# Two-layer attention kernel on one core: the hi and lo parts of the setup's products and the first statistics take other places in the engines' queues

## The chip, the core and the metric

The kernel runs on one core of one Trainium2 chip. The metric is the device time of one execution in microseconds (us); the median of several executions is compared. The engines named in the profile are PE (TensorE, matrix products; PEld is its weight load), ACT (ScalarE), DVE (VectorE), POOL (GpSimd) and SP (SyncE, which issues all the transfers here). Each engine works through its own queue of instructions in program order and waits at semaphores. Memory on the chip is SBUF (128 partitions) and PSUM, to which TensorE writes.

## The reference, cut to what matters

The input x is 8 x 512 x 32 x 32, in float32. Two attention layers follow each other:

```python
# layer 0
hn = group_norm(x, gn1_scale, gn1_bias)              # 32 groups of 16 channels
qkv = einsum('bchw,oc->bohw', hn, w_qkv) + b_qkv     # 8 heads of 64 channels, 1024 positions
a = softmax(q^T k / sqrt(64)) v                      # per batch element and head
x = x + group_norm(einsum(a, w_proj) + b_proj, gn2_scale, gn2_bias)
# layer 1
w_qkv, w_out = g * v / norm(v, axis=1)               # weight normalisation, rows
qkv = einsum('oc,bcn->bon', w_qkv, x); qkv = qkv / (rms over channels + 1e-4)
h = softmax(q^T k * 512**-0.5) v                     # one head of 512 channels
out = (x + einsum('oc,bcn->bon', w_out, h)) / sqrt(2)
```

## The kernel before, in words

**Arithmetic.** Large products are made from split operands: a float32 value is stored as a hi part, rounded by a copy to the type float32r, and a lo part, which is the value minus the hi part. A product then takes three passes, hi x hi, hi x lo and lo x hi. ScalarE makes hi parts and VectorE lo parts, so each split is two instructions on two engines, the second waiting for the first.

**The loop.** After a setup, eight batch elements run one after the other in `body(b, last)`. Each engine has such a body with the same steps. TensorE projects q and k (line 560), then v, runs 64 score steps with transposes and values around them, the output projection, and the products of layer 1. The body of the change's kernel is the same.

**The setup on TensorE** (lines 451 to 479) makes three products of the weights of layer 1, each in four units `i = 0..3` of 128 rows, in plain float32, which TensorE takes as two instructions per matmul in the trace:
- first product (line 458): v_qkv blocks 8 to 11 with wo, 8 instructions of 512 columns a unit. Unit 0 and 1 go at once; unit i from 2 on waits for `s_prod_lo >= i - 1`, that is for the lo part of unit i - 2, which frees the buffer `big[i % 2]`.
- second product (line 465): blocks 0 to 3 with 4 to 7, also 8 instructions a unit. It first waits for all 12 weight blocks to be normalised; unit i waits for `s_prod_lo >= 3 + i`.
- the group means of the first x (line 469), which wait for `s_gn_mean >= 1`, the end of the channel statistics.
- third product (line 473), 24 instructions a unit, narrower from unit to unit (512, 384, 256, 128 columns); unit i waits for `s_prod_lo >= 7 + i`. After its unit 0 come the group variances (lines 444 and 446).
Before the first body TensorE waits for all twelve lo parts and for the normalised x.

**The setup on ScalarE** (lines 759 to 796): the sums of squares of the weight blocks 8 to 11, then of blocks 0 to 7 (`square_sums`, line 746), then `product_hi(0)`, four pairs of q/k weight splits (line 772, two instructions each), `product_hi(1)`, the two long splits of the v and output weights into W0 and W1 (line 778), `product_hi(2)`, `product_hi(3)` and so on. `product_hi(i)` (line 748, its instruction at line 754) waits for unit i, counted over all three products, and copies the hi part out of PSUM.

**The setup on VectorE** (lines 1041 to 1139): the scaling of blocks 8 to 11, `product_lo(0)` (line 1048, its instruction at line 1053), the scaling of blocks 0 to 7 (line 1065), which waits for GpSimd's power of all twelve sums of squares (line 942), then four pairs of q/k lo parts (line 1072), `product_lo(1)`, the lo parts of W0 and W1 (line 1080), `product_lo(2)`, `product_lo(3)`, `product_lo(4)`. Then it waits for x (`s_x_next`) and makes the channel statistics of four blocks (lines 1087 to 1090, three instructions each), with `product_lo(5)`, `(6)` and `(7)` after the first three. Group means, variances and coefficients, the normalised x (line 1110) and its lo part (line 1116) follow.

**SP's queue** (lines 312 to 350, then its body): the loads of the weights; after `s_split_lo >= 4` the load of x into XA (line 327), whose space held the q/k weights; after `s_split_lo >= 6` the load of v_out (line 329), then the stores of the first group (d_qk[0], d_wp and, after the first product, d_u, line 338). SP waits for these, reloads the first q/k weights (line 340) and stores the second group (d_wv, the other d_qk, d_m). It waits for that group (line 346), stores d_g (line 349), waits for it, and goes on to its body: the second q/k weights (line 372) and the stack loads (`stack_head`, line 364), which wait for the q and k of the batch (`s_nat_ready`) and which the first scores wait for. One stack is six loads of 256 KB.

```python
pe.wait_ge(s_prod_lo, i - 1)              # first product, unit i >= 2 (line 457)
pe.wait_ge(s_prod_lo, KB + i - 1)         # second product, unit i (line 463)
group_means(1, ops[0][:, 0:KB], every, None, s_gn_first)     # line 469
pe.wait_ge(s_prod_lo, 2 * KB + i - 1)     # third product, unit i (line 471)
sp.wait_ge(s_split_lo, PAIRS)             # ahead of the load of x (line 326)
```

Of the kernel before, what the change touches and what calls it, by code (L numbers as in the profile page):

```python
# [20 lines left out]
KB = C // P  # L21
# [12 lines left out]
ACT = mybir.ActivationFunctionType  # L34
# [50 lines left out]
def build(nc, x, wv_t, wp_t, wqk_t, v_qkv, v_out, wo_t, vecs, consts, out):  # L85
    ctx = ExitStack()
    with ctx:
        def sb(name, shape, dt=f32):
            return ctx.enter_context(nc.sbuf_tensor(name, shape, dt))
# [4 lines left out]
        def sem(name):  # L94
            return ctx.enter_context(nc.semaphore(name))
# [9 lines left out]
        X = sb("X", [P, KB, N])  # L105
# [7 lines left out]
        W = [sb("W0", [P, 4096], f32r), sb("W1", [P, 4096], f32r)]  # L113
# [68 lines left out]
        s_split_hi = sem("split_hi")  # L182
# [81 lines left out]
        def w1_block(j, start=0, stop=HALF):  # L264

            return PB[:, j // 2, HALF * (j % 2) + start:HALF * (j % 2) + stop]

        def qk_part_of(tile, part):

            return tile.rearrange("p (k n) -> p k n", k=KB)[:, :, P * part:P * part + P]  # L270

        def wqk_stage(i):
            return XA[:, (2, 3, 0, 1)[i], :]

        def product_stage(i):

            return (ST[:, 4:8, :].rearrange("p a n -> p (a n)"), PT[:, :, :, :].rearrange("p a h n -> p (a h n)"),
                    ST[:, 0:4, :].rearrange("p a n -> p (a n)"))[i]

        def product_parts(i):  # L280

            k = i % KB
            if i // KB == 0:
                return [(slice(0, HALF), 1.0)]
            if i // KB == 1:
                return [(slice(0, HALF), SCALE1)]

            return [(slice(P * k, P * k + P), 1.0)] + ([(slice(P * k + P, HALF), 2.0)] if k < KB - 1 else [])
# [451 lines left out]
        def _(act):  # L740
            act_fn = nc.scalar.activation

            def square_sums(n, src, col):
                if n > 1:
                    act.wait_ge(s_square_sum, n - 1)
                act_fn(RB[:, 0:HALF], src, ACT.Square, accum_out=ssq[:, col:col + 1]).then_inc(s_square_sum, 1)

            def product_hi(i):
                act.wait_ge(s_big_full, i + 1)
                if i == 2 * KB:  # L750
                    act.wait_ge(s_const_set, 1)
                for cols, factor in product_parts(i):
                    at = HALF * (i % KB)
                    last = act_fn(product_stage(i // KB)[:, at + cols.start:at + cols.stop], big[i % 2][:, cols],
                                  ACT.Copy, scale=factor)
                last.then_inc(s_prod_hi, 1)
# [6 lines left out]
            act.wait_ge(s_in_l1, 8 * 16)  # L763
            for j in range(8):
                square_sums(j + 5, w1_block(j), j)
            for i in range(PAIRS):
                if i == 0:
                    product_hi(0)
                if i % 2 == 0:
                    act.wait_ge(s_in_qk[i // 2], 32)  # L770
                for part, factor in ((0, SCALE0), (1, 1.0)):
                    last = act_fn(qk_part_of(VT[:, 2 * i, :], part), qk_part_of(wqk_stage(i), part),
                                  ACT.Copy, scale=factor)
                last.then_inc(s_split_hi, 1)
            product_hi(1)
            act.wait_ge(s_in_l0, 32)
            for w, src in ((W[0], X[:, 0:2, :]), (W[1], X[:, 2:4, :])):
                act_fn(w[:, 0:2048], src.rearrange("p a n -> p (a n)"), ACT.Copy).then_inc(s_split_hi, 1)
            product_hi(2)
            product_hi(3)  # L780
            for i in range(KB):
                product_hi(KB + i)
            act.wait_ge(s_in_vout, 16)
# [246 lines left out]
        def _(dve):  # L1030
# [4 lines left out]
            def link(instruction):  # L1035

                instruction.then_inc(s_dve_step, 1)
                links[1] += 1
                dve.wait_ge(s_dve_step, links[0] + links[1])
# [8 lines left out]
            def product_lo(i):  # L1048
                dve.wait_ge(s_prod_hi, i + 1)
                for cols, factor in product_parts(i):  # L1050
                    at = HALF * (i % KB)
                    stage = product_stage(i // KB)
                    last = V.scalar_tensor_tensor(stage[:, 2048 + at + cols.start:2048 + at + cols.stop],  # L1053
                                                  big[i % 2][:, cols], factor,
                                                  stage[:, at + cols.start:at + cols.stop].bitcast(f32),
                                                  ALU.mult, ALU.subtract)
                last.then_inc(s_prod_lo, 1)

            for n, rows in ((1, range(8, 12)), (2, range(0, 8))):  # L1060
                dve.wait_ge(s_norm_pow, n)
                cols = slice(rows.start, rows.stop)
                link(V.tensor_tensor(wscale[:, cols], rnorm[:, cols], g_l1[:, cols], ALU.mult))
                for j in rows:
                    V.tensor_scalar(w1_block(j), w1_block(j), wscale[:, j:j + 1], None, ALU.mult)\
                     .then_inc(s_w_normed, 1)
                if n == 1:
                    product_lo(0)
            for i in range(PAIRS):
                dve.wait_ge(s_split_hi, i + 1)  # L1070
                for part, factor in ((0, SCALE0), (1, 1.0)):
                    last = V.scalar_tensor_tensor(qk_part_of(VT[:, 2 * i + 1, :], part),
                                                  qk_part_of(wqk_stage(i), part), factor,
                                                  qk_part_of(VT[:, 2 * i, :], part).bitcast(f32),
                                                  ALU.mult, ALU.subtract)
                last.then_inc(s_split_lo, 1)
            product_lo(1)
            for i, (w, src) in enumerate(((W[0], X[:, 0:2, :]), (W[1], X[:, 2:4, :]))):
                dve.wait_ge(s_split_hi, i + PAIRS + 1)
                V.tensor_tensor(w[:, 2048:4096], src.rearrange("p a n -> p (a n)"), w[:, 0:2048].bitcast(f32),  # L1080
                                ALU.subtract).then_inc(s_split_lo, 1)
            product_lo(2)
            product_lo(3)
            product_lo(KB)

            def channel_stats(k):
                V.bn_stats(stats[:, k, 0:6], XA[:, k, 0:HALF])
                link(V.bn_stats(stats[:, k, 6:12], XA[:, k, HALF:N]))
                own_wait(dve)
                return V.bn_aggr(mv[:, k, :], stats[:, k, :])  # L1090
# [28 lines left out]
            dve.wait_ge(s_x_next, 16)  # L1119
            for k in range(KB):  # L1120
                last = channel_stats(k)
                if k < KB - 1:
                    product_lo(KB + k + 1)
            last.then_inc(s_gn_mean, 1)
            dve.wait_ge(s_gn_mean, 1)
            dve.wait_ge(s_gn_first, 1)
            group_dev(ops[0][:, 0:KB], mv[:, :, 0], every)
# [299 lines left out]
```

## Time and profile before

| what | value |
|---|---|
| median of 3 executions | 3530.38 us |
| lowest and highest | 3525.94 and 3533.14 us |
| the profiled execution's own time | 3528.0 us |
| its span, first to last instruction | 3526.2 us |
| mean granted clock of TensorE | 0.998 |
| TensorE busy (matmuls) | 3462.6 us, 98% of the span |
| VectorE / ScalarE / GpSimd busy | 2077.1 / 1825.4 / 1083.3 us |
| first matmul of the first batch | 83.42 us |

### The profile page before, as it was taken

How to read it: one execution, taken by the hardware profiler on the slowest of the kernel's cores; microseconds unless marked ns; L12 is line 12 of the kernel's file. 1: busy time of each engine (PE TensorE's matmuls, PEld its weight loads, DVE VectorE, ACT ScalarE, POOL GpSimd, SP SyncE). 2: the span in 40 equal slices, each digit the busy share in tenths (PEclk: the TensorE clock that was granted, in tenths of full speed). 3: DMA queues.
4: the chain of work that ended last, by engine and by line, in shares of the span. 5: the costliest groups of instructions: out<-in, count | busy, mean ns of one | idle time of the engine just before them, and what ended most of it. 6: DMA issues, size and time to landing. Idle time of an engine off the chain costs nothing.

```text
span 3526.2 us, 52658 instructions
## 1 busy us (share of the span) xinstructions
PE 3462.6 (98%) x17360; PEld 2835.9 (80%) x17360; DVE 2077.1 (59%) x3388; ACT 1825.4 (52%) x3074; POOL 1083.3 (31%) x947
## 2 busy tenths in 40 slices
PE   7999999999999999999999999999999999999999
PEld 3888788887888788887878878788787887888878
DVE  4677446773377734786347854478444884457742
ACT  3577126762278522784237832378323882247822
POOL 0245213442034410354104531145211452114521
PEclk9999999999999999999999999999999999999999
DMA  8512215312244113341033311342203422142210
GB/s 310 157 39 58 108 43 138 74 48 84 66 115 96 41 69 97 85 96 72 36 121 81 76 72 43 114 96 61 84 37 109 96 61 84 43 133 65 60 48 24
DMA packets 63520, 294.41 MB, mean 83 GB/s; under 512 B 9201, under 2 KB 9457, under 8 KB 52465
## 3 DMA queue, kind: packets, MB, share of 16 engines
q1 hardware_dynamic: 63216, 290.65, 28.1%
q8 instruction: 156, 2.56, 0.3%
q14 instruction: 148, 1.20, 0.1%
HBM read 158.49 MB, written 31.46 MB: 54 GB/s over the span
## 4 chain that ended last, share of the span: by engine, by line
PE 87%; issue 6%; DVE 3%; ACT 2%; POOL 2%; DMA 0%; SPq 0%; ACTq 0%; DVEq 0%; POOLq 0%
PE big L430 29%; PE tps L529 14%; PE big L556 12%; PE ops L542 12%; PE ops L702 10%; PE big L626 6%; PE big L473 1%; PE ops L430 1%; ACT PB L827 1%; PE big L594 1%; DVE XA L1247 1%; POOL XA L967 1%; DVE HL L1252 0%; DVE small L1175 0%; PE big L465 0%
## 5 line engine op out<-in xcount | busy, mean ns | idle before, releaser
L957 POOL TENSOR_SCALAR PB<-PB,small 128x1024 f32<-128x1024 f32 x576 | 648.1, 1126 | 1304.3 <-DVE small L1181 1293.4
L833 ACT ACTIVATE PT<-tps 128x512 fp32r<-128x512 f32 x1088 | 601.2, 597 | 251.7 <-PE tps L529 248.5
L1186 DVE TENSOR_TENSOR PT<-tps,PT 128x512 fp32r<-128x512 f32 x1088 | 693.1, 678 | 39.0 <-ACT PT L833 38.6
L1175 DVE TENSOR_REDUCE small<-big 128x1 f32<-128x1024 f32 x512 | 624.8, 1220 | 63.2 <-PE big L556 59.9
L529 PEld LDWEIGHTS tps<-ident,PB 128*128 128x128 f32 x4608 | 527.1, 140 | 125.0 <-DVE PT L1186 56.0
L529 PE MATMUL tps<-ident,PB 128*128 128x128 f32 x4608 | 618.0, 275 | 8.9 <-DVE PT L1186 6.1
L827 ACT ACTIVATE PB<-big,small 128x1024 f32<-128x1024 f32 x512 | 572.2, 1118 | 73.1 <-DVE small L1175 70.2
L542 PE MATMUL ops<-PT,VT 128*128 128x512 f32 x2048 | 599.3, 415 | 0.0
L556 PE MATMUL big<-ST 128*128 128x512 f32 x2048 | 555.4, 393 | 10.9 <-ACT PB L827 10.9
L556 PEld LDWEIGHTS big<-ST 128*128 128x128 f32 x2048 | 382.1, 188 | 101.8 <-ACT PB L827 19.9
L542 PEld LDWEIGHTS ops<-PT,VT 128*128 128x128 f32 x2048 | 346.2, 189 | 47.0 <-DVE PT L1186 5.0
L430 PE MATMUL big<-HH,W 128*128 128x512 f32 x1024 | 333.9, 391 | 1.7 <-DVE ST L1053 1.1
L1167 DVE SCALAR_TENSOR_TENSOR ST<-big,vec,ST 128x512 fp32r<-128x512 f32 x128 | 96.1, 751 | 326.6 <-ACT ST L819 326.6
L819 ACT ACTIVATE ST<-big,vec 128x512 fp32r<-128x512 f32 x128 | 88.2, 689 | 303.8 <-PE big L430 303.8
L430 PEld LDWEIGHTS big<-HH,W 128*128 128x128 f32 x1024 | 192.3, 188 | 45.5 <-issue 4.4
L1322 DVE CUSTOM_DVE_ANT_0 PB<-big,RB 128x1024 f32<-128x1024 f32 x64 | 78.4, 1225 | 240.4 <-PE big L430 240.4
L967 POOL TENSOR_TENSOR XA<-RB 64x512 f32<-64x512 f32 x128 | 163.9, 1281 | 142.8 <-ACT RB L844 141.6
L1018 POOL TENSOR_SCALAR small<-small 128x1 f32<-128x1 f32 x64 | 16.9, 265 | 616.6 <-DVE small L1322 607.6
L430 PE MATMUL big<-HL,W 128*128 128x512 f32 x512 | 200.0, 391 | 0.0
L430 PE MATMUL big<-W,HH 128*128 128x512 f32 x640 | 197.1, 389 | 0.0
L702 PE MATMUL ops<-PT,VT 128*128 128x512 f32 x768 | 188.3, 394 | 0.0
L626 PE MATMUL big<-ST,W 128*128 128x512 f32 x720 | 183.2, 395 | 1.2 <-ACT XA L885 1.1
(157 smaller groups left out, 4659.2 us busy)
## 6 DMA issues: line engine op xcount, KB each, us to landing
ST<-ST SPq DMA_DIRECT2D x384, 256.0 KB, 4.9
W<-d_qk SPq DMA_DIRECT2D x32, 1024.0 KB, 5.2
XA<-in_x SPq DMA_DIRECT2D x8, 2048.0 KB, 7.7
X<-in_x SPq DMA_DIRECT2D x8, 2048.0 KB, 10.6
W<-d_wp SPq DMA_DIRECT2D x8, 2048.0 KB, 12.2
W<-d_g SPq DMA_DIRECT2D x8, 2048.0 KB, 12.2
W<-d_m SPq DMA_DIRECT2D x8, 2048.0 KB, 7.7
W<-d_u SPq DMA_DIRECT2D x8, 2048.0 KB, 10.3
```

What stands on the lines that cost most here:

```text
L430: last = mm(dst, stat(sp_, k), mov(mp_, k), start=(i == 0), stop=(i == n - 1))
L529: last = nc.tensor.transpose(tps[n % 2][:, P * t:P * t + P], PB[:, 4 * (u % 2) + t, P * s:P * s + P], ident[:])
L542: last = mm(ops[u % 2][:], VT[:, s, P * (u // 2):P * (u // 2) + P], pt_slot(u, s)[:, part, :], start=(s == 0 and part == 0), stop=(s == 7 ...
L556: last = mm(t[:, cols], stack("q", head)[:, tok:tok + P], stack(kind, head)[:, cols], start=(i == 0), stop=(i == 1))
L626: last = mm(t[:, cols], w_full[slot][:, wp, j, P * k:P * k + P], x1(xp, j)[:, cols], start=(j == 0 and i == 0), stop=(j == (k if slot == 0 ...
L702: last = mm(ops[use % 2][:], VT[:, s, col:col + P], ptb[:, pp, :], start=(s == 0 and i == 0), stop=(s == 7 and i == 2))
L827: act_fn(PB[:, i, :], t[:], ACT.Exp, bias=negmax[:, i:i + 1], accum_out=rowsum[:, i:i + 1])\
L833: act_fn(pt_slot(u, s)[:, 0, :], tps[n % 2][:], ACT.Copy).then_inc(s_pt_hi, 1)
L957: nc.gpsimd.tensor_scalar(PB[:, i, :], PB[:, i, :], rinv[:, i:i + 1], 1.0, ALU.mult, ALU.mult)\
L967: nc.gpsimd.tensor_tensor(XA[rows, pair, HALF * c:HALF * c + HALF], RB[rows, 0:HALF], RB[rows, HALF:N], ALU.add).then_inc(s_a_done, 1)
L1175: V.tensor_reduce(negmax[:, i:i + 1], tile(("s", 4 * u + tb))[:], axis=AX.X, op=ALU.max, negate=True).then_inc(s_row_max, 1)
L1186: V.tensor_tensor(pt_slot(u, s)[:, 1, :], tps[n % 2][:], pt_slot(u, s)[:, 0, :].bitcast(f32), ALU.subtract).then_inc(s_pt_ready, 1)
```

## The change

All of it lies in the setup. No instruction, wait or transfer is added or taken away. On ScalarE `product_hi(0)` goes ahead of the last three of the eight squares, `product_hi(1)` ahead of the q/k splits, `product_hi(2)` ahead of the third pair, `product_hi(3)` between the two long splits. On VectorE `product_lo(1)` goes ahead of the q/k lo parts, `product_lo(2)` ahead of the third pair, `product_lo(3)` between the long lo parts. Of the lo parts that stood between the channel statistics, one (`KB + 1`) stays, after the second block instead of the first; the other two follow the statistics.

```diff
             for j in range(8):
                 square_sums(j + 5, w1_block(j), j)
+                if j == 4:
+                    product_hi(0)
+            product_hi(1)
             for i in range(PAIRS):
-                if i == 0:
-                    product_hi(0)
+                if i == 2:
+                    product_hi(2)
                 if i % 2 == 0:
                     act.wait_ge(s_in_qk[i // 2], 32)
...
                 last.then_inc(s_split_hi, 1)
-            product_hi(1)
             act.wait_ge(s_in_l0, 32)
-            for w, src in ((W[0], X[:, 0:2, :]), (W[1], X[:, 2:4, :])):
-                act_fn(w[:, 0:2048], src.rearrange("p a n -> p (a n)"), ACT.Copy).then_inc(s_split_hi, 1)
-            product_hi(2)
+            act_fn(W[0][:, 0:2048], X[:, 0:2, :].rearrange("p a n -> p (a n)"), ACT.Copy).then_inc(s_split_hi, 1)
             product_hi(3)
+            act_fn(W[1][:, 0:2048], X[:, 2:4, :].rearrange("p a n -> p (a n)"), ACT.Copy).then_inc(s_split_hi, 1)
...
                 if n == 1:
                     product_lo(0)
+            product_lo(1)
             for i in range(PAIRS):
+                if i == 2:
+                    product_lo(2)
                 dve.wait_ge(s_split_hi, i + 1)
...
                 last.then_inc(s_split_lo, 1)
-            product_lo(1)
             for i, (w, src) in enumerate(((W[0], X[:, 0:2, :]), (W[1], X[:, 2:4, :]))):
+                if i:
+                    product_lo(3)
                 dve.wait_ge(s_split_hi, i + PAIRS + 1)
...
-            product_lo(2)
-            product_lo(3)
             product_lo(KB)
...
             for k in range(KB):
                 last = channel_stats(k)
-                if k < KB - 1:
-                    product_lo(KB + k + 1)
+                if k == 1:
+                    product_lo(KB + 1)
             last.then_inc(s_gn_mean, 1)
+            product_lo(KB + 2)
+            product_lo(KB + 3)
```

## Rows read from the trace of the kernel before

**Rows 1.** The page, its chain that ended last: shares by engine.
```profile
PE 87%; issue 6%; DVE 3%; ACT 2%; POOL 2%; DMA 0%; SPq 0%; ACTq 0%; DVEq 0%; POOLq 0%
```

**Rows 2.** Chain of waits in order of time, to 130 us: start us, us, what.
```profile
15.04 0.73 ACT RB L746 x2
...
20.31 0.73 ACT RB L746 x2
...
31.71 5.23 PE big L458 x8
36.94 13.85 PE big L465 x32
...
54.19 12.10 PE big L473 x24
...
83.42 27.52 PE big L430 x120
```

**Rows 3.** Timeline of ScalarE: start us, us, instruction, idle before and releaser.
```profile
20.94 0.58 ACT L754 ACTIVATE ST<-big 128x512 fp32r<-128x512 f32 x1
21.41 4.25 ACT L772 ACTIVATE VT<-XA 128x512 fp32r<-128x512 f32 x8
...
26.05 3.70 ACT L778 ACTIVATE W<-X 128x2048 fp32r<-128x2048 f32 x2
...
36.98 0.60 ACT L754 ACTIVATE ST<-big 128x512 fp32r<-128x512 f32 x1 [6.74 <-PE big L458]
```

**Rows 4.** Timeline of VectorE.
```profile
26.16 4.89 DVE L1072 SCALAR_TENSOR_TENSOR VT<-XA,VT 128x512 fp32r<-128x512 f32 x8
30.98 0.68 DVE L1053 SCALAR_TENSOR_TENSOR ST<-big,ST 128x512 fp32r<-128x512 f32 x1
31.58 4.47 DVE L1080 TENSOR_TENSOR W<-X,W 128x2048 fp32r<-128x2048 f32 x2
...
41.75 0.68 DVE L1087 BATCH_NORM_STATS2 small<-XA 128x6 f32<-128x512 f32 x1
...
43.17 0.21 DVE L1090 BATCH_NORM_AGGREGATE small<-small 128x2 f32<-128x12 f32 x1
```

**Rows 5.** Windows: from:to, us, PE, PEld, DVE, ACT, POOL busy, PEclk, DMA, GB/s.
```profile
31.70:34.80 3.10, 3.09 (x4) 1.51 (x5) 3.10 (x2) 0.00 (x0) 0.00 (x0) 0.50 0.79 255
...
50.60:53.80 3.20, 0.18 (x1) 0.00 (x1) 2.09 (x4) 2.89 (x8) 0.00 (x0) 1.00 0.92 394
...
55.50:58.50 3.00, 3.00 (x5) 1.35 (x4) 0.00 (x0) 0.00 (x0) 0.00 (x0) 0.50 0.35 46
```

**Rows 6.** Timeline of the weight loads, the eighth and ninth matmul of line 458 near.
```profile
16.99 0.34 PEld L458 LDWEIGHTS big<-PB 128*128 128x128 f32 x1 [0.52 <-issue]
...
18.23 0.19 PEld L458 LDWEIGHTS big<-PB 128*128 128x128 f32 x1 [0.24 <-issue]
```

**Rows 7.** Timeline of SP's issues.
```profile
31.08 0.38 SPq L327 DMA_DIRECT2D XA<-in_x  x1
...
83.00 0.32 SPq L349 DMA_DIRECT2D d_g<-ST  x1
89.51 0.32 SPq L372 DMA_DIRECT2D W<-d_qk  x1
96.21 13.46 SPq L364 DMA_DIRECT2D ST<-ST  x12
```

**Rows 8.** Transfers issued from 31 to 33 us: KB, us to landing.
```profile
XA<-in_x SPq DMA_DIRECT2D x1, 2048.0 KB, 7.9
```

**Rows 9.** The page, its DMA issues over the whole span: KB each, median us to landing.
```profile
ST<-ST SPq DMA_DIRECT2D x384, 256.0 KB, 4.9
...
X<-in_x SPq DMA_DIRECT2D x8, 2048.0 KB, 10.6
```

**Rows 10.** TensorE's waits from 300 us on, and a window behind one of them.
```profile
PE big L626 <- DVE HL L1252: 14.6, 8, 1.8
...
366.10:370.00 3.90, 3.89 (x17) 3.24 (x18) 3.15 (x2) 0.00 (x0) 3.90 (x2) 1.00 0.18 17
```

## The prediction, made before any run of the changed kernel

> **What bounds the kernel now.** I read the chain of waits first, because it tells whether time won in the setup can reach the end. TensorE is 87% of it [rows 1], and in order of time it says where the setup's length comes from [rows 2]: ScalarE's squares, the weight normalisation that hangs on them, VectorE's splits of the q/k weights up to 31.05 [rows 4], the fourth unit of the first product (TensorE, 31.71), the second product (36.94 to 50.79), then nothing on TensorE until 54.19, the third product, and the first batch from 83.42. From there TensorE hardly waits, so I take a microsecond won before 83.42 as a microsecond of the whole.
>
> So TensorE has two large holes. The first ends at 31.71. That unit needs the buffer that product_lo(1) frees. product_lo(1) stands behind eight split instructions on VectorE, and product_hi(1) behind eight on ScalarE [rows 3, 4]. The second, from 50.79, ends with the statistics of x, whose last quarter follows product_lo(7) [rows 2]. The granted clock adds a price to each hole: it is 0.50 (1.2 GHz) from 31.7 to 34.8, and again from 55.5 to 58.5, though it was still full in the hole at 50.6 to 53.8 [rows 5]. The weight loads show the two spacings: 0.85 us a matmul at the low level (the next load is at 17.80), 0.43 at 2.4 GHz (next at 18.66) [rows 6]. A unit of eight therefore takes 3.44 us, and each low stretch costs some four matmuls times 0.43, 1.7 us.
>
> **The change, step by step.** It adds no instruction and no transfer; it moves hi/lo parts and statistics. I rebuild the times with durations as spacings: ScalarE square 0.75 (15.04 to 20.31 in seven), hi part 0.47, split 0.52, long split 1.85 [rows 2, 3]; VectorE lo part 0.60, q/k split 0.60, long split 2.2 [rows 4]; a hi part starts 0.27 after its unit's last matmul; TensorE starts 0.73 after the start of the lo part that frees it (product_lo(1) starts at 30.98) [rows 2 to 4].
> 1. product_hi(0) now sits before the last three squares. The spacings put the end of unit 0 at 18.56 [rows 6], so it starts at 18.83, with ScalarE free at 18.80. It pushes the squares back 0.5, and with them the power on GpSimd and the scaling of the eight blocks: its end goes from 26.16 [rows 4] to 26.66. That is the only new wait ahead of the scaling. The gain in unit 2 is 0.3 (start 22.0 instead of 22.29, as unit 1 ends then).
> 2. product_lo(1) follows the scaling: 26.66. Unit 3 starts at 27.39, not 31.71, and ends at 30.83: 4.3 won, and 1.7 more if the clock holds over a hole of 1.95 us.
> 3. product_hi(2) waits on ScalarE until 25.7 with splits 2 and 3 queued behind it; those end at 28.25, still before VectorE asks (30.3). product_lo(2) starts at 29.67, and the second product's unit 0 at 30.83.
> 4. VectorE's q/k splits end at 32.75, 1.7 later than now (scaling 0.5, two lo parts 1.2). SP's queue stands behind them: the load of x goes out at 32.78, not 31.08 [rows 7]. It lands 7.9 later [rows 8], at 40.7.
> 5. product_hi(3) waits for unit 3 until 31.1; the copy of W1 behind it ends at 33.4, and VectorE wants it at 35.5, so it costs nothing. product_lo(3) stands behind the long split of W0: 34.91. This is a new hole: unit 1 of the second product needs it, and starts at 35.64 instead of 34.27. W1's lo part ends at 37.74, so v_out and the first stores go out about 1.75 later than now.
> 6. product_lo(4) starts at 37.74, and unit 2 runs 39.08 to 42.52. Statistics 0 and 1 wait for x: 40.7 to 43.8 (1.54 each, from the start at 41.75, the aggregate's at 43.17 and 0.12 behind it [rows 4]). product_lo(5) follows at 43.8, and unit 3 can start only at 44.5: a new hole of 2.0 us. It ends at 47.94.
> 7. Statistics 2 and 3 end at 47.5, product_lo(6) starts there. The group means and the third product start at 48.25 instead of 54.04: 5.8 won. product_lo(7), now last, ends at 49.5 and nobody needs it until TensorE's second unit of that product, near 58.5.
> 8. Without the low stretch at 55.5, the third product's unit 0 is 1.7 shorter. After it every step keeps its distance to the one before.
> Sum: 5.8 + 1.7 = 7.5 us. The first batch starts at 75.9 instead of 83.42.
>
> **What must stay hidden.** SP waits for the first stores (about 58.9 instead of 57.2), for the second group (about 82.4), then stores d_g at 82.5 (83.00 now) and issues the q/k load at 89.0 (6.5 later, as now) [rows 7]. The stack loads could start at 88.7 and start at 89.4. The first scores then want them at 103.3 (110.8 now, 14.5 behind the first issue at 96.21). Six issues at 1.12 and 4.9 to land [rows 7, 9] give 99.9; up to 2.6 more where the 1 MB q/k load (at about 400 GB/s) is still under way. That makes 102.5: covered by 0.8, a small margin.
>
> **The unknown costs.** The first is the clock. Nothing here shows my 2 us holes in the setup. The nearest row below is the wait of 1.8 us in each batch, after which the clock stays at 1.00 [rows 10]; the nearest above is the hole of 3.4 us, after which it fell [rows 2, 5]. My 2.0 lies next to 1.8, so I take no fall and keep 1.7 us as the other end. The Trainium skill (TensorE: Matmul & The Clock Gate, section HAM oscillation) speaks against this change: bursts of matmuls with waits between them can fall back to the half clock again and again. By that rule the sum would be 5.9, by the row it is 7.5. The second is the landing of x. Loads of the same size take 7.9 here and 10.6 for X in the batches [rows 8, 9]; I take 7.9, since the surroundings are the same. Each microsecond later is one off the gain.
>
> **The time.** The profiled execution spans 3526.2 and took 3528.0, 2.4 under the median. A span of 3518.7 and a time of 3520.5 would correspond to a median of 3530.38 - 7.5 = 3522.9.
>
> **Rivals.**
> - Clock falls in the hole at 42.5 (0.20): unit 3 takes 1.7 longer and ends at 49.6, the third product starts at 49.9, gain 4.1 + 1.7 = 5.9 (rounded up from 5.84): 3524.5. For it: three holes within 20 us. Against: 1.8 us holes hold [rows 10]. A fall in unit 3 of the first product costs only 0.3, as the new hole behind it absorbs the rest.
> - x lands late (0.14): at 10.6 everything from step 6 is 2.7 later, the hole grows to 4.7 and the clock probably falls in it: gain 3.3 to 4.8, about 3526.5.
> - x lands early (0.07): with x there at 38.4, statistics end at 45.2 and the third product starts at 46.1: gain 9.6, 3520.8. No load of this size here is that fast.
> - Stack loads late (0.07): this is the mechanism that could end slower. Its place is the first scores of batch 0. It decides from 103.3 on, eats the gain at one microsecond each, and turns the result slower once they land after 110.8. If the second group of stores took 12 us more, they would land at 114.5: 3534.1. Against: that group's bytes are the same, and nothing shares the engines with it that does not now.
>
> **How the numbers follow.** The forecast has 0.52. A measurement of this kernel can tell about 0.2%, 7.1 us, from no change; three runs spread over 7.2. The forecast of 7.5 sits almost on that line: six in ten of its chance count as faster (0.31), plus the early x (0.07) and a little of the fallen clock (0.02): faster 0.40. Slower needs most of the last rival's tail: 0.03. The rest, 0.57, is within. The range goes from the early x with some scatter, 3518.5, to the late x with some, 3529.0.
>
> **What would show it.** In the profile of the changed kernel: unit 3 of the first product at 27.4; x issued at 32.8; holes on TensorE near 34.3 (1.4 us) and 42.5 (2.0 us); third product at 48.2; clock 1.00 from 18 on; batch 0 at 75.9; no wait of the first scores for a stack load. A clock of 0.5 after 42.5, or x landing after 41, would make the forecast wrong in size; a batch start at 75.9 with an end unchanged would make its main premise wrong.

## The result, and the profile after

The changed kernel has a median of 3520.74 us (15 executions, 3519.58 to 3524.91), the kernel before 3528.80 in the same set (15 executions, 3525.03 to 3533.14). The ratio is 0.9979 with a 95% interval of 0.9971 to 0.9987: 8.1 us less between the medians, against 7.5 forecast. The profiled execution spans 3518.8 us, where 3518.7 was forecast.

The timeline of TensorE in the changed kernel answers to [rows 2]. Columns: start us, us, instruction, and in brackets the idle time before it with its releaser. First, three lines of the same view of the kernel before:

```profile
31.71 5.23 PE L458 MATMUL big<-PB 128*128 128x512 f32 x8 [5.72 <-DVE ST L1053]
...
53.83 0.36 PE L437 MATMUL ops<-small,gavg 128*128 128x4 f32 x2 [3.05 <-DVE small L1090]
54.04 12.24 PE L473 MATMUL big<-PB 128*128 128x512 f32 x24
```

and then the changed kernel:

```profile
26.98 3.70 PE L458 MATMUL big<-PB 128*128 128x512 f32 x8 [1.85 <-DVE ST L1054]
30.52 3.60 PE L465 MATMUL big<-PB 128*128 128x512 f32 x8
35.20 7.13 PE L465 MATMUL big<-PB 128*128 128x512 f32 x16 [1.08 <-DVE ST L1054]
43.99 3.70 PE L465 MATMUL big<-PB 128*128 128x512 f32 x8 [1.67 <-DVE PT L1054]
47.53 0.28 PE L437 MATMUL ops<-small,gavg 128*128 128x4 f32 x2
47.67 10.55 PE L473 MATMUL big<-PB 128*128 128x512 f32 x24
...
75.35 0.49 PE L430 MATMUL big<-HH,W 128*128 128x512 f32 x1 [1.09 <-DVE ST L1054]
```

The long holes before 31.71 and before the group means are gone, and three short ones stand in their place: before unit 3 of the first product, before unit 1 and before unit 3 of the second. The first unit of the third product (24 matmuls, line 473) takes 10.55 instead of 12.24 (12.10 in the chain of [rows 2], which counts it from 54.19): no low clock behind it. The first batch starts at 75.35 instead of 83.42, 8.07 earlier.

VectorE shows what ends the last hole: the load of x, then two statistics, and product_lo(5) behind them (its timeline, against [rows 4]).

```profile
40.24 0.69 DVE L1090 BATCH_NORM_STATS2 small<-XA 128x6 f32<-128x512 f32 x1 [2.30 <-DMA XA<-in_x]
...
43.30 0.64 DVE L1054 SCALAR_TENSOR_TENSOR PT<-big,PT 128x512 fp32r<-128x512 f32 x1
...
46.91 0.64 DVE L1054 SCALAR_TENSOR_TENSOR PT<-big,PT 128x512 fp32r<-128x512 f32 x1
```

Part of the 8.07 is given back a little later. SP's timeline (against [rows 7]):

```profile
32.37 0.38 SPq L327 DMA_DIRECT2D XA<-in_x  x1
...
82.00 0.32 SPq L349 DMA_DIRECT2D d_g<-ST  x1
90.38 0.32 SPq L372 DMA_DIRECT2D W<-d_qk  x1
90.90 13.98 SPq L364 DMA_DIRECT2D ST<-ST  x12
```

and TensorE's first scores of batch 0:

```profile
103.92 1.19 PE L556 MATMUL big<-ST 128*128 128x512 f32 x4 [1.09 <-DMA ST<-ST]
```

TensorE is 8 us earlier, but the stores of the setup are not: d_g goes out at 82.00 (83.00 before), since SP still waits for the second group (the twelfth lo part was done at 74.9). It takes 8.4 us to SP's next issue, not 6.5, so the stack loads start at 90.90 and the first scores wait 1.09 us for them. They start at 103.92 against 110.76: 6.8 of the 8.07 are left there.

### The profile page after: what moved, and what is told of

Read it like the earlier page. It is cut to its first block, busy times and chain, and to the rows that moved or that the text cites. A ratio compares the mean times of both kernels' runs of the same rounds, so it can differ in the third digit from the quotient of the medians.

```text
span 3518.8 us, 52658 instructions
## 1 busy us (share of the span) xinstructions
PE 3457.8 (98%) x17360; PEld 2832.2 (80%) x17360; DVE 2077.7 (59%) x3388; ACT 1826.7 (52%) x3074; POOL 1086.0 (31%) x947
## 3 DMA queue, kind: packets, MB, share of 16 engines
q8 instruction: 156, 2.56, 0.3%
## 4 chain that ended last, share of the span: by engine, by line
PE 85%; issue 6%; DVE 3%; ACT 2%; DMA 2%; POOL 2%; SPq 0%; ACTq 0%; DVEq 0%; POOLq 0%
PE big L430 28%; PE tps L529 14%; PE big L556 12%; PE ops L542 12%; PE ops L702 10%; PE big L626 6%; PE ops L430 1%; DVE XA L1252 1%; ACT PB L828 1%; PE big L594 1%; DMA d_m<-PT 1%; DMA d_u<-ST 1%; POOL XA L968 1%; DVE HL L1257 0%; DVE small L1180 0%
## 5 line engine op out<-in xcount | busy, mean ns | idle before, releaser
L1180 DVE TENSOR_REDUCE small<-big 128x1 f32<-128x1024 f32 x512 | 625.1, 1221 | 63.7 <-PE big L556 60.3
## 6 DMA issues: line engine op xcount, KB each, us to landing
W<-d_u SPq DMA_DIRECT2D x8, 2048.0 KB, 10.2
```

The lines of the kernel that those rows point to most:

```text
L1180: V.tensor_reduce(negmax[:, i:i + 1], tile(("s", 4 * u + tb))[:], axis=AX.X, op=ALU.max, negate=True).then_inc(s_row_max, 1)
```

## The experiments

Each run was timed against the kernel before; the sets are named with their own median of before. The last table puts the starts of all profiled executions together.

**The changed kernel again** (set 1, before 3527.87).

> The changed kernel again, as the yardstick of this set. Theory (order of the queues plus the clock): first batch of TensorE starts near 75.4 us, third product near 47.7, no stretch at the low clock after the first 17 us, some 7 to 8 us under the kernel before; the first scores of batch 0 wait about 1 us for the stack loads. Rival (the gain of the setup is partly chance in the landing of transfers): the start of the first batch moves by over 1 us against 75.35.

Measured: 3521.88 us (3518.93 to 3522.64), ratio 0.9982 (0.9973 to 0.9991), 6.0 us less. The third product starts at 47.25, the first batch at 74.93, and the first scores wait 0.98 us for the stack loads. The setup repeats within half a microsecond, yet its span is 3520.8, 2.0 longer than the first profile's. So the difference between two executions does not come from the setup; what it is comes below.

**The old order of the statistics put back** into the changed kernel:

```diff
-                if k == 1:
-                    product_lo(KB + 1)
+                if k < KB - 1:
+                    product_lo(KB + k + 1)
             last.then_inc(s_gn_mean, 1)
-            product_lo(KB + 2)
-            product_lo(KB + 3)
```

> The changed kernel with the old order of statistics and lo parts of the second product; the moves of the first product stay. Theory (two holes, each of its own order, both joined by the landing of x): x lands near 40.3, product_lo(5) follows the first statistics at 41.8 and unit 3 of the second product starts at 42.5 or before, with no hole; it ends at 45.9. product_lo(7) then waits for it and puts the last statistics off to 47.4 to 48.9; third product at about 49.4, after a hole of 3.4 us, in which the clock may fall (1.7 us). First batch at 77.1 without and 78.8 with the fall: 1.7 to 3.4 us slower than the changed kernel, 4.6 to 6.3 faster than before. Rival 1 (the moves of the first product carry all): same as the changed kernel. Rival 2 (the statistics carry all): as before, 83.4.

Measured: 3523.23 us, ratio 0.9986 (0.9977 to 0.9995), 4.6 less than before. TensorE's timeline:

```profile
36.09 10.86 PE L465 MATMUL big<-PB 128*128 128x512 f32 x24 [1.08 <-DVE ST L1054]
49.99 0.36 PE L437 MATMUL ops<-small,gavg 128*128 128x4 f32 x2 [3.05 <-DVE small L1093]
50.21 12.24 PE L473 MATMUL big<-PB 128*128 128x512 f32 x24
```

Units 1 to 3 of the second product run without a hole, the hole before the group means is back at its old 3.05 us, and the next unit takes 12.24: the low clock is back with it (0.72 in the window from 49 to 52, 0.71 from 52 to 55). The first batch starts 63.9 us after ScalarE's first square of the second set of blocks, the changed kernel's 60.5: 3.4 later, the forecast's case with the fall. Both rivals fall: it lies between the changed kernel and the one before.

**The new order of the statistics alone**, in the kernel before: the same lines the other way round.

> The kernel before with the new order of the statistics alone. Theory: the first product's last unit stays at 31.7 and the second product at 36.9; product_lo(5) is ready at 45.4, before unit 2 ends, so there is no new hole; unit 3 ends at 50.6, the statistics at 48.5, so the third product starts at about 50.8 instead of 54.0, and the low clock at 55.5 is gone (1.7 us). First batch at about 78.5, 4.9 us faster than before. Rival 1 (the first product's part carries all): 83.4, no change. Rival 2 (the statistics carry all): 75.4.

Measured: 3523.30 us, ratio 0.9989 (0.9980 to 0.9998), 4.6 less. TensorE's timeline:

```profile
38.03 13.90 PE L465 MATMUL big<-PB 128*128 128x512 f32 x32
51.76 0.28 PE L437 MATMUL ops<-small,gavg 128*128 128x4 f32 x2
51.90 10.55 PE L473 MATMUL big<-PB 128*128 128x512 f32 x24
```

The second product leaves no hole behind it and the clock stays up. All starts are 1.1 later than forecast because the weights landed later here; counted from the first square the first batch is at 63.5 against 68.4 before, the 4.9 forecast and between the two rivals. Each half of the change is therefore worth about five alone (68.4 to 63.9 is 4.5) and the two together 7.9, not 9.4: in the whole, the second product runs ahead of x, and part of what the first half wins is waited away there.

**The price of the clock alone**: three matmuls that nobody reads in the hole of the kernel before.

```diff
+            for n in range(3):
+                mm(ops[1][:], w1_block(n, 0, P), w1_block(4), start=True, stop=True)
             pe.wait_ge(s_in_consts, 32)
             group_means(1, ops[0][:, 0:KB], every, None, s_gn_first)
```

> The kernel before with three matmuls whose results nobody reads put into the hole of TensorE ahead of the group means (2.6 us of work in a hole of 3.1). Nothing else moves, so it prices the clock alone. Theory: the third product still starts at 54.0, but its first unit runs wholly at 2.4 GHz and is 1.7 us shorter; first batch at 81.7, 1.7 us faster than before. Rival (the low clock at 55.5 is not due to the hole, or costs nothing on the path): first batch at 83.4, no change.

Measured: 3526.77 us (3524.28 to 3528.07), ratio 0.9997 (0.9988 to 1.0006), which by itself tells nothing. The timeline does:

```profile
50.19 2.74 PE L469 MATMUL ops<-PB 128*128 128x512 f32 x6
53.40 0.36 PE L437 MATMUL ops<-small,gavg 128*128 128x4 f32 x2 [0.47 <-DVE small L1092]
53.62 10.55 PE L475 MATMUL big<-PB 128*128 128x512 f32 x24
```

The third product starts no earlier, counted from the first square (39.0 in both), and its first unit takes 10.55 instead of 12.24. The first batch starts 1.7 earlier (66.7 against 68.4). Of the change's 7.9, 1.7 is the clock's.

**Is the new hole before unit 3 on the path?** (set 2, before 3527.22) product_lo(5) ahead of the wait for x:

```diff
+            product_lo(KB + 1)
             dve.wait_ge(s_x_next, 16)
             for k in range(KB):
                 last = channel_stats(k)
-                if k == 1:
-                    product_lo(KB + 1)
```

> The changed kernel with product_lo(5) ahead of the wait for x instead of behind the second statistics. Theory (the third product is set by the landing of x and four statistics plus the one lo part between them): product_lo(5) runs at about 39.5, so unit 3 of the second product follows unit 2 at about 42.1 with no hole; but the statistics still end only 0.6 us earlier, so the third product and the first batch come 0.55 us earlier, no more. Rival (the hole of 1.7 us ahead of unit 3 is on the path): 1.7 us earlier.

Measured: 3521.39 us, ratio 0.9982 (0.9973 to 0.9991). TensorE's timeline:

```profile
26.77 5.40 PE L458 MATMUL big<-PB 128*128 128x512 f32 x8 [3.39 <-DVE ST L1054]
32.00 13.90 PE L465 MATMUL big<-PB 128*128 128x512 f32 x32
46.60 0.35 PE L437 MATMUL ops<-small,gavg 128*128 128x4 f32 x2 [0.70 <-DVE small L1093]
47.06 10.57 PE L473 MATMUL big<-PB 128*128 128x512 f32 x24
```

The hole before unit 3 is gone and the first batch comes 0.3 earlier (60.2 against 60.5), not 1.7: the rival falls, the statistics of x set the third product. The forecast 0.55 was too high; the statistics start at 40.31, behind product_lo(5), which itself waited for its hi part until 39.70. One thing is new: unit 3 of the first product takes 5.40 us, the low clock, after a hole shown as 3.39 (1.85 in the first profile of the changed kernel, 2.56 in its repeat, both followed by 3.70). It cost nothing: the third product starts 32.5 behind the first square, and 32.4 in "both" below, which has the same order and kept the clock (unit 3 in 3.70). The waits behind that unit took it up. The first scores did not gain: they start at 103.78, after 1.51 us of waiting for the stack loads.

**Who keeps the first scores waiting?** First SP's order, with the store of d_g ahead of the wait for the second group:

```diff
-            sp.wait_ge(s_stored_l0, 80)
-            sp.sem_inc(s_ld_wv, 16)
             sp.wait_ge(s_prod_lo, 3 * KB)
             sp.dma_start(d_g[:], product_stage(2).bitcast(f32)).then_inc(s_stored_g, 16)
+            sp.wait_ge(s_stored_l0, 80)
+            sp.sem_inc(s_ld_wv, 16)
```

> The changed kernel with SP's store of d_g issued as soon as the twelfth lo part is there, ahead of the wait for the second group of stores. Nothing before the first batch moves. Theory (the first scores wait for stack loads that stand behind SP's store of d_g and its 8.4 us to the next issue): d_g goes out near 75, is there near 87, SP is free for the stack loads when q and k are ready at 88.5, they land some 2.5 us earlier and the wait of 1.0 us before the first scores is gone: 1 us faster than the changed kernel. Rival (the stacks are late through their own share of the transfer engines, not through SP): the wait of about 1 us stays.

Measured: 3520.31 us (3518.05 to 3522.82), ratio 0.9980 (0.9971 to 0.9989). SP's timeline:

```profile
76.11 0.32 SPq L347 DMA_DIRECT2D d_g<-ST  x1
87.39 0.32 SPq L372 DMA_DIRECT2D W<-d_qk  x1
89.33 13.40 SPq L364 DMA_DIRECT2D ST<-ST  x12
```

and TensorE's first scores, with nothing ahead of them to wait for:

```profile
103.88 1.07 PE L556 MATMUL big<-ST 128*128 128x512 f32 x4
```

Here the weights landed 1.2 us later than in the first profile, so the first batch starts at 76.53. The scores follow it by 27.35 us, as in the kernel before (110.76 - 83.42 = 27.34), against 28.57 in the changed kernel.

Then the q/k load behind the first stack, in every batch:

```diff
-                sp.dma_start(w_qk(1)...).then_inc(ld_qk[1], 16)
                 stack_head(b, 0, 0)
+                sp.dma_start(w_qk(1)...).then_inc(ld_qk[1], 16)
                 stack_head(b, 0, 1)
```

> The changed kernel with the 1 MB load of the second q/k weights behind the first stack in SP's queue, in every batch. Theory: the stack loads of batch 0 start 0.5 us earlier and have the transfer engines to themselves, so they land 0.5 to 2.6 us earlier and the wait of 1 us goes: up to 1 us faster than the changed kernel. Rival (the load does not compete with them): the wait shrinks by the 0.5 us of its issue at most.

Measured: 3519.64 us (3518.64 to 3521.23), ratio 0.9979 (0.9970 to 0.9988). The wait is gone here too: first batch at 76.56, scores at 103.87.

```profile
82.37 0.32 SPq L349 DMA_DIRECT2D d_g<-ST  x1
91.16 5.75 SPq L364 DMA_DIRECT2D ST<-ST  x6
96.95 1.22 SPq L373 DMA_DIRECT2D W<-d_qk  x1
```

The stacks start no earlier than in the changed kernel (91.16 against 90.90), with d_g as late as there. But this run alone does not tell the two causes apart: its first batch was 1.2 later, which alone covers a wait of 1.09. Only the early d_g shows more than that, since the stack loads there waited for q and k (from 87.39 to 89.33), not for SP.

**Both edits, product_lo(5) first and d_g early:**

> The changed kernel with product_lo(5) ahead of the wait for x and the early store of d_g together. Theory: 0.55 plus 1.0, the first batch 0.55 earlier and no wait for the stacks: about 1.5 us faster than the changed kernel, some 9 under the kernel before. Rival: no better than the better one of its parts.

Measured: 3520.11 us (3518.28 to 3521.63), ratio 0.9978 (0.9969 to 0.9987). First batch at 74.71, about as early as in the repeated changed kernel (74.93), scores at 102.06, no wait for the stacks. That is 1.3 us before the repeated changed kernel's 103.38, and it shows that the early d_g takes the wait away at the early start also. The medians of this set are all within 1.8 us and do not order the variants.

**Where the scatter comes from.** The batches after the setup differ from one profile to the next. Windows of 50 us over the batches of the kernel before, those whose granted clock was under 1 (the third column from the right; one that reaches past the last matmul is left out):

```profile
780.00:830.00 50.00, 48.02 (x215) 39.29 (x214) 24.99 (x38) 10.23 (x12) 16.47 (x8) 0.97 0.39 148
2080.00:2130.00 50.00, 48.17 (x209) 38.74 (x208) 20.65 (x29) 9.17 (x10) 14.48 (x7) 0.97 0.28 106
3330.00:3380.00 50.00, 47.83 (x219) 37.50 (x218) 29.57 (x49) 18.18 (x26) 15.90 (x11) 0.97 0.12 43
```

A closer look at the first (timeline of TensorE, then a window):

```profile
795.68 0.56 PE L626 MATMUL big<-HH,W 128*128 128x512 f32 x1 [1.83 <-DVE HL L1252]
```

```profile
796.60:800.00 3.40, 3.40 (x11) 2.66 (x10) 2.31 (x2) 0.00 (x0) 3.33 (x2) 0.59 0.21 35
```

This is the very hole of [rows 10], which the prediction took for proof that 1.8 us do not bring the clock down. In the same profile it fell behind that hole in 3 batches of 8. The next run fills the hole in every batch:

```diff
+                for n in range(7):
+                    mm(ops[1][:], HH[:, 0, 0:P], HH[:, 0, 0:HALF], start=True, stop=True)
                 x1_block(2)
```

> The changed kernel with seven matmuls whose result nobody reads in the wait of 1.8 us that TensorE has in every batch ahead of the third block of layer 1's input (about 1.6 us of work in the hole). Theory (the scatter between executions comes from this hole, after which the granted clock falls in 2 to 5 of the 8 batches, at about 1.6 us each): no stretch at the low clock in the batches, all eight of them 429.6 us long, some 3 to 6 us faster than the changed kernel and a narrower spread. Rival (the falls have another cause than the hole): they stay, and the extra matmuls cost nothing or up to 0.2 us a batch.

Measured (set 3, before 3527.26): 3516.08 us (3514.81 to 3520.08), ratio 0.9968 (0.9956 to 0.9979), mean clock 1.000.

```profile
356.93 1.75 PE L653 MATMUL ops<-HH 128*128 128x512 f32 x7
358.93 0.50 PE L626 MATMUL big<-HH,W 128*128 128x512 f32 x1 [0.25 <-DVE HL L1259]
```

No such window is under 1 any more, and the matmul behind the hole comes at the same distance to the first scores (358.93 - 103.42 = 255.51 against 359.51 - 103.92 = 255.59): the seven matmuls cost nothing. The rest of the span from the first scores on is 3410.9 us, against 3414.9 in the changed kernel (2 falls) and 3417.4 in its repeat (4 falls): 1.6 to 2.0 us a fall. All twelve profiles of the table below line up by this count. From the first scores on they take 3410.9 and 3411.0 with no fall, 3413.8 to 3414.9 with two, 3415.1 to 3415.8 with three and 3416.6 to 3417.4 with four: 1.4 to 2.0 us a fall.

**All three together:**

> The changed kernel with product_lo(5) ahead of the wait for x, the early store of d_g and the seven idle matmuls together. Theory: the three add up, near 3515 us, some 12 under the kernel before. Rival: as fast as the version without the idle matmuls, 3520.

Measured: 3515.27 us (3514.80 to 3517.16), ratio 0.9965 (0.9950 to 0.9979), 12 us under before and the fastest version; the 0.8 over the one before it is within the scatter. First batch at 75.77, scores at 103.10, no wait.

All profiled executions, in us; "first square" is ScalarE's start on the second set of weight blocks, which hangs on a load, and "falls" counts the batches with a stretch at the low clock:

| kernel | first square | third product | first batch | first batch - first square | falls | span |
|---|---|---|---|---|---|---|
| before | 15.04 | 54.04 | 83.42 | 68.4 | 3 | 3526.2 |
| changed | 14.77 | 47.67 | 75.35 | 60.6 | 2 | 3518.8 |
| changed, again | 14.62 | 47.25 | 74.93 | 60.3 | 4 | 3520.8 |
| statistics put back | 15.66 | 50.21 | 79.58 | 63.9 | 2 | 3520.7 |
| statistics alone | 16.12 | 51.90 | 79.58 | 63.5 | 3 | 3522.4 |
| before, hole filled | 14.61 | 53.62 | 81.30 | 66.7 | 2 | 3522.6 |
| product_lo(5) first | 14.56 | 47.06 | 74.79 | 60.2 | 3 | 3519.6 |
| d_g early | 15.92 | 48.86 | 76.53 | 60.6 | 4 | 3521.0 |
| stack first | 16.12 | 48.88 | 76.56 | 60.4 | 3 | 3519.0 |
| both | 14.55 | 46.98 | 74.71 | 60.2 | 4 | 3518.7 |
| changed, batch hole filled | 14.44 | 47.18 | 74.86 | 60.4 | 0 | 3514.3 |
| all three | 15.44 | 48.07 | 75.77 | 60.3 | 0 | 3514.1 |

The changed kernel's setup up to the first batch is also that of d_g early, stack first and the filled batch hole; the mean of the first four of these five is 60.5.

## Why the prediction was right, point by point

**The order of the queues (steps 1 to 7): right, to 0.6 us.** Forecast and measured starts: unit 3 of the first product 27.39 and 26.98, the load of x 32.78 and 32.37, unit 1 of the second product 35.64 and 35.20, the first statistics 40.7 and 40.24, unit 3 of the second product 44.5 and 43.99, the third product 48.25 and 47.67. All are early by 0.4 to 0.6. Of this, 0.27 is the first square, which started at 14.77 instead of 15.04, and 0.15 the slip of the scaling against it, 0.35 (23.07 - 14.77 = 8.30, before 22.99 - 15.04 = 7.95) where step 1 has 0.5. Both new holes stood where they were put. x landed 7.9 us after its issue, as taken.

**The clock's 1.7 (step 8): right in size, its evidence wrong.** The price is shown by the filled hole, 1.7. But "I take no fall" rested on a single instance of the 1.8 us hole in the batches, where eight stood in the trace; three of the eight were followed by a fall. In the new setup holes it did not fall in either profile of the changed kernel; in product_lo(5) first, d_g early and stack first it fell with the first of them, which was longer there (3.39, 3.50 and 3.15; unit 3 took 5.40, 5.40 and 5.09 instead of 3.70), and cost nothing, as the rival's text had it ("a fall in unit 3 of the first product costs only 0.3"); with the statistics put back it held over 3.16. In the run with the statistics alone it fell behind a hole of 1.91 in the first product (its next unit took 5.40). The hole before unit 3 of the second product, 1.36 to 1.67 in five profiles, brought no fall in any. The chance of 0.20 was a guess on one sample, not a count. The Trainium skill's page (TensorE: Matmul & The Clock Gate, section HAM oscillation), that bursts with waits between them can fall back again and again, fits the trace better than my row did: 2 to 4 stretches of low clock an execution behind one recurring 1.8 us hole. But the waits in that section's example are longer than this hole and than the 2.0 us of the prediction's, so the 5.9 that the prediction drew from it went further than the page does. For the sum of this change it made no difference.

**"Covered by 0.8, a small margin": this step failed.** The stack loads were late by 1.09 us. The mis-sized term is SP's distance from the store of d_g to its next issue: 6.5 was taken from before, 8.4 was measured (8.7 in the repeat, 8.4 in product_lo(5) first). The 1.9 more turn the margin of 0.8 into a wait of 1.1 (the store and the point from which the scores want their stacks both came half a microsecond earlier than forecast, which cancels). That the store now goes out at once behind the second group is not the reason. With the statistics alone it does so too (SP issues it at 80.34, when the twelfth lo part had been done since 79.1), and the distance is 6.5. What does differ is a load of instructions. Here is what the transfer engines moved between the two issues (queue: packets, MB, share of the 16 engines). With the statistics alone, from 80.34 to 86.86 (the kernel before has the same 144 packets from 83.00 to 89.51):

```profile
q1 hardware_dynamic: 144, 2.10, 76.1%
```

In the changed kernel, from 82.00 to 90.38:

```profile
q1 hardware_dynamic: 144, 2.10, 59.9%
q8 instruction: 1, 0.02, 0.7%
```

The second line is one packet of instructions, 16 KB. It falls between 87.4 and 88.1, at the end of the store. The last large packet of the store begins only between 88.1 and 88.6, alone:

```profile
q1 hardware_dynamic: 1, 0.02, 12.7%
```

The stretch holds no packet of instructions in the three kernels with 6.5 (before, statistics alone, before with the hole filled). It holds one in all six others in which the store waits for the group: 7.1 us to the next issue with the statistics put back, 8.4 to 8.8 in the rest. That the load holds the store up is argued from this coincidence; no run moves it by itself. The prediction's argument against this rival, that "nothing shares the engines with it that does not now", did not count such loads. The rival named the right place and started from the right point (103.3 forecast, 102.83 measured); its price was one microsecond, not eleven. The early d_g takes it away.

**The sum.** 8.07 at the first batch, less 1.2 at the first scores (27.34 behind it before, 28.57 now) and 0.2 on the way to the hole of batch 0, leaves 6.6 there (359.51 against 366.11); the rest of 7.4 in the span is the batches' own scatter, with one fall fewer in this profile. Two figures of the prediction are slightly off and bear on nothing: the late x with a fall would gain 3.1, not 3.3 (7.5 - 2.7 - 1.7), and [rows 6] show 0.81 us to the load at 17.80, since the clock rises in between; the low spacing is 0.85 from 16.14 to 16.99. That the span met its forecast to 0.1 us is luck: a setup half a microsecond earlier than forecast and that scatter made up for the wait of 1.1. The medians say 8.1 in one set and 6.0 in the other, around the forecast 7.5. Whether it passes 7.1 is therefore a matter of the set; the interval of the first, 4.6 to 10.2 us, holds both answers, and 0.40 against 0.57 was a fair statement.

## What to carry to other kernels

Where hi and lo parts of several products share two in-order queues with long side work, write down which instruction frees the next buffer and put it directly behind what it needs; then look at what the moved work had been hiding, here a load of x that went out 1.3 us later and stores that did not get earlier. A gain in a setup arrives in the loop only as far as the transfers that the loop waits for move with it. And before taking a hole as harmless to the clock, look at all its instances: filling one hole of 1.8 us a batch with idle matmuls was worth more than half of this whole change. Between "both" and "all three", which differ in nothing else, the medians fall by 4.8 us (3520.11 and 3515.27, with the kernel before at 3527.22 and 3527.26 in their sets), against 6.0 and 8.1 for the change.

## What was not expected of the hardware

- The same hole of 1.8 us, eight times an execution, is followed by a stretch at the lower of the two levels in 2 to 4 batches of 8 (ten profiles), not the same ones from profile to profile. At 1.4 to 2.0 us each this explains differences of 2 to 4 us between executions of one kernel. With the hole cut to 0.25 us there was none in 16 batches of two profiles.
- The landing of the same weight loads moved the whole setup by up to 1.7 us between profiles (first square 14.44 to 16.12).
- SP's distance from the 2 MB store of d_g to its next issue was 6.5 us in three kernels and 7.1 to 8.8 in six. Only in the six does a 16 KB load of instructions fall into it. Whose instructions these are, and whether the load is the cause, is open.
- Why a fall follows some of the holes and not others is open; no run here tells it.
